# First expert layer of a two-layer adaLN kernel: indirect transfers without the waits on the shared expert

## The reference

```python
def _L0_ffn_ref(x, up, gate, down, router, w_up_s, w_gate_s, w_down_s):
    x_ = x.reshape(b * t, c)
    logits = x_ @ router.T
    idx = jnp.argmax(logits, axis=-1)            # one of 8 experts per token
    ...
    h = jax.nn.silu(g) * u                       # 256 hidden features per expert
    ye = jnp.einsum('ebh,ech->ebc', h, down)
    y = jnp.einsum('ebc,be->bc', ye, onehot)     # the token's own expert
    ys = jax.nn.silu(x_ @ w_gate_s.T) * (x_ @ w_up_s.T) @ w_down_s.T   # shared expert
    return (y + ys).reshape(b, t, c)
```

## Time and profile before

| | us |
|---|---|
| median of 3 runs | 1029.12 |
| the runs | 1025.5, 1029.12, 1032.63 |
| the profiled execution, its own time | 1024.61 |
| its span, first to last instruction | 1022.8 |
| mean granted TensorE clock | 0.978 of full speed |

### The profile page before, as it was taken

One profiled execution on the slowest core, in us unless ns is written; L12 is line 12 of the kernel. 1 busy time (PEld: TensorE's weight loads), 2 busy tenths in 40 slices (PEclk: granted clock), 3 DMA queues, 4 the chain that ended last, 5 costly groups with the idle time before them and its releaser, 6 DMA issues.

```text
span 1022.8 us, 21590 instructions
## 1 busy us (share of the span) xinstructions
PE 940.9 (92%) x7416; PEld 605.7 (59%) x7416; DVE 637.5 (62%) x2103; ACT 554.9 (54%) x1078; POOL 453.8 (44%) x682
## 2 busy tenths in 40 slices
PE   8999999999989989999994988889997999999996
PEld 3566777777654223334642886456664644499994
DVE  4789998999816967854642444768773643344444
ACT  6536667676657555565421554567775522255551
POOL 1146776777642946610064553045551044323331
PEclk9999999999999989999997999999999899999999
DMA  6600000000020000040012234000000010111115
GB/s 215 221 2 3 3 2 2 3 2 3 2 93 1 0 1 1 0 165 0 4 48 65 72 83 169 17 2 2 2 2 1 1 32 29 48 44 50 49 32 175
DMA packets 32602, 42.02 MB, mean 41 GB/s; under 512 B 6960, under 2 KB 26800, under 8 KB 31632
## 3 DMA queue, kind: packets, MB, share of 16 engines
q1 hardware_dynamic: 27952, 31.26, 9.8%
q0 software_dynamic: 4544, 9.38, 2.8%
HBM read 29.16 MB, written 16.66 MB: 45 GB/s over the span
## 4 chain that ended last, share of the span: by engine, by line
PE 72%; issue 14%; ACT 5%; DVE 5%; DMA 2%; POOL 1%; SPq 0%; DVEq 0%; POOLq 0%; ACTq 0%
PE PS L693 6%; PE PS L434 5%; PE PS L476 5%; PE PS L676 5%; PE PS L683 5%; PE PS L447 4%; PE PS L330 3%; PE PS L339 3%; PE PS L629 3%; PE PS L627 3%; PE PS L636 2%; PE PS L536 2%; PE PS L427 2%; PE PS L802 2%; PE PS L783 2%
## 5 line engine op out<-in xcount | busy, mean ns | idle before, releaser
L911 ACT ACTIVATE pw<-PS 128x384 f32<-128x384 f32 x256 | 111.5, 488 | 71.5 <-PE PS L456 68.9
L1587 POOL TENSOR_SCALAR_AFFINE_SELECT pw<-pw 128x256 f32<-128x256 f32 x256 | 105.1, 434 | 75.0 <-ACT pw L911 73.1
L1185 DVE CUSTOM_DVE_ANT_0 PS<-PS,above 128x256 f32<-128x256 f32 x256 | 115.8, 452 | 23.0 <-PE PS L427 22.8
L1653 POOL DMA_INDIRECT token_rows<-xnb,slot_in x78 | 75.0, 962 | 119.3 <-ACT xnb L1014 112.9
L1639 POOL TENSOR_TENSOR XS<-XS,N 128x512 f32<-128x512 f32 x64 | 81.2, 1288 | 55.4 <-DVE N L1263 34.7
L434 PE MATMUL PS<-kf,qm 32*128 32x256 f32 x512 | 103.6, 426 | 0.5 <-POOL qm L1596 0.5
L1439 DVE TENSOR_TENSOR rsb<-sqb,PS 128x256 f32<-128x256 f32 (+1 forms) x78 | 43.3, 555 | 96.7 <-PE PS L683 39.4
L1609 POOL TENSOR_SCALAR_AFFINE_SELECT pw<-pw 128x256 f32<-128x256 f32 x128 | 56.1, 472 | 68.6 <-ACT pw L1059 68.6
L1187 DVE CUSTOM_DVE_ANT_0 PS<-PS,above 128x128 f32<-128x128 f32 x256 | 84.6, 331 | 0.0
L1596 POOL TENSOR_SCALAR qm<-qs,qmask 128x256 f32<-128x256 f32 x64 | 59.7, 934 | 44.2 <-ACT kf L892 44.2
L997 ACT ACTIVATE sqb<-PS 128x512 f32<-128x512 f32 x48 | 28.7, 597 | 90.2 <-PE PS L627 80.3
(11 more groups left out here) (213 smaller groups left out, 2383.5 us busy)
## 6 DMA issues: line engine op xcount, KB each, us to landing
sorted_rows<-empty_rows_dram SPq DMA_DIRECT2D x2, 2535.0 KB, 14.4
slot_in<-sorted_rows SPq DMA_DIRECT2D x78, 65.0 KB
N<-token_rows SPq DMA_DIRECT2D x16, 256.0 KB, 4.6
X<-xT_dram SPq DMA_DIRECT2D x8, 256.0 KB, 5.7
ATT<-gate_dram SPq DMA_DIRECT2D x1, 2048.0 KB
XS<-down_dram SPq DMA_DIRECT2D x1, 2048.0 KB
H<-up_dram SPq DMA_DIRECT2D x1, 2048.0 KB
out_dram<-X SPq DMA_DIRECT2D x8, 256.0 KB, 3.6
```

The lines of the kernel that those rows point to most:

```text
L911: nc.scalar.activation(pw[:, w % 2, j + n, :], PS[:, A_PST + (2 * v + n) % 3, 0:3 * P], ACT.Exp).then_inc(a_p, 1)
L1185: nc.vector.tensor_tensor_reduce(x[:, 0:SEQ], x[:, 0:SEQ], above[:, :], 1.0, -3e38, ALU.add, ALU.max, mx[:, t // 8 % 2, 1, j, g:g + 1])
L1587: m = nc.gpsimd.affine_select(x[:, :, SEQ * k:SEQ * k + P], x[:, :, SEQ * k:SEQ * k + P], [[0, 2], [1, P]], ALU.is_ge, 0.0, base=0, channe ...
L1653: nc.gpsimd.indirect_dma_start(token_rows[l][:, :], bass.IndirectOffsetOnAxis(slot_in[:, r, D:D + 1].bitcast(mybir.dt.int32), 0), slot_out ...
```

## The change

In the first layer (l is 0) the 32 indirect transfers no longer wait for `s_hidden`. In the second (l is 1) the waits are as they were. The waits for `pos` and for the fill of `sorted_rows`, ahead of the loop, stay in both.

```diff
                 pool.wait_ge(q["pos"], 1)
                 pool.wait_ge(r_fill, 32)
                 for n in range(TILES):
-                    pool.wait_ge(q["s_hidden"], n * 7 // 8 + 3 if l else min(n * 2 // 3 + 1, NCH * c["NH"] + 2 - LATE))
+                    if l:
+                        pool.wait_ge(q["s_hidden"], n * 7 // 8 + 3)
                     nc.gpsimd.indirect_dma_start(sorted_rows[l][:, :], bass.IndirectOffsetOnAxis(pos[:, n:n + 1], 0),
                                                  rows[l][:, n, :], None).then_inc(q["dispatched"], 16)
```

## The result

| | before | changed |
|---|---|---|
| median, us | 1027.03 (6 runs) | 1038.58 (6 runs) |
| lowest to highest, us | 1024.24 to 1032.63 | 1034.91 to 1041.59 |
| profiled execution's span, us | 1022.8 | 1035.8 |
| ratio with its 95% interval | 1 | 1.0111 (1.0086 to 1.0137) |

The changed kernel is slower by 11.5 us where 4.4 us less was forecast. That is not the whole result. In one it takes 1023 to 1028 us and the sends of the first layer's routed part are about 1.75 us apart; in the other it takes 1014 to 1015 us and they are 1.44 us apart. I call them the **tight** and the **easy** condition. The traces of before and after above are of the tight one. In the easy condition the change makes the kernel faster, by 0.6% (0.9936, 0.9923 to 0.995), much as forecast.

What follows compares the result with a forecast made beforehand. The prediction took GpSimd's first-layer string of indirect transfers to set the time while TensorE idles 13.5 us; the median of 1029.12 us less 4.4 us, waits, side effects and clock at nothing, gave 1024.7 us, range 1018 to 1031.

Steps and rivals of the forecast that it cites:

- The string: GpSimd's 32 first-layer indirect transfers: without waits 1.265 us apart, last start at 548.26 instead of 552.69, gain 4.4 us.
- The third rival: First-layer waits cost more than thought, idle 0.30 us between transfers goes too: 13.7 us gain, 1015.4 us; chance 0.05.
- What is next: TensorE's transposition at line 667 starts at 552.5 instead of 556.95; its idle time falls from 13.5 to 9.1 us.
- Side effects of the earlier transfers: More transfers lie beside the first layer's shared expert, 27 instead of 24 before 543 us; cost nothing.
- The cover of 6.2 us: Before line 667's transposition: its other conditions are met by 546.3, it starts at 552.5; slipping shared steps have 6.2 us.
- The first rival: First layer's unpaced string slows, eighteen steps at 1.77 us: net 4.7 us slower, 1033.8 us; chance 0.06.
- The rule of the port pair: Skill's rule that VectorE holding the shared ports blocks GpSimd's descriptor writes, stretching the string; the sum took no stretch.
- The clock: TensorE's clock after its idle time before line 667: up to 1.6 us saved or lost, taken as nothing.

Runs made afterwards that it cites:

- x_plain: Changed kernel with the first layer's 32 transfers made plain ones in token order, sorting left out; 0.9926 of the kernel before, tight condition.
- z_spaced: Changed kernel with a GpSimd fill of 256 zeros per partition between the first layer's transfers; 1.0005 of the kernel before, tight condition.
- z_late: Changed kernel with the first layer's string started only when s_hidden is 8, then free; 1.0085 of the kernel before, tight condition.
- x_second: Kernel before with the second layer's transfers unpaced, the first layer's still paced; 1.0242 of the kernel before, tight condition.
- e8_half_pace: Kernel before with first-layer waits on s_hidden at n // 2 + 1 instead of min(2n/3 + 1, 16); 0.9998 of it, tight condition.

## Why the prediction was wrong

Point by point.

**The string.** Right. 39.4 us in both conditions, 2.3 us from the last start to the first slot's load. The third rival (the waits cost more) is out: spacing stayed at 1.265 us.

**What is next.** Right in the easy condition: 13.4 us of waiting became 9.0. There the kernel gains 0.6% (0.9936) and 0.55% (0.9945), 5.6 to 6.5 us against my 4.4. The traces show just the 4.4 us up to line 667 (48.0 to 43.6), so the last 1 to 2 us lie elsewhere; what they come from stays open. 4.4 us lies inside the interval of the second measurement and outside that of the first.

**Side effects of the earlier transfers: "Cost: nothing, by three rows."** This is the step that failed: a term that the sum put at 0 us came to 15 us. Up to line 667 the changed kernel was to gain 4.4 us, and it lost 10.9. I showed by the DMA share, by the bytes and by the distance of chosen multiplies that the unbroken string does not disturb the shared expert, and each of those rows is true. But I took the multiplies of 513 and 515 us, in the first 7 us of the string, and of 539 and 541, where it was paced, and left out the ones between. VectorE's multiply at 527.37 is 1.2 us late right behind the only 14 unbroken transfers that the trace has. In the tight condition ScalarE and VectorE start 1.4 to 13.4 us late from 16 to 19 us of unbroken string on, and the 14 steps end 22 us later, counted from the string's start (57.1 us behind it, where it was 34.6). The cover of 6.2 us that I named for such a slip was eaten several times over.

**The first rival** had the right place ("nothing measured beyond 14") and the wrong victim: I let the transfers slow each other down to 1.77 us. They never left 1.265. The price of 1033.8 us fell short of 1038.6. No rival let the string hold up the engines that compute. The row to follow was the late multiply at 527.37.

**The rule of the port pair.** The Trainium skill, page "SBUF — State Buffer", section "Who interferes with whom", says that where an instruction of VectorE contends with GpSimd, whoever issues first holds the shared port pair for the whole instruction and the other blocks, and that TensorE and ScalarE never wait on anyone. The trace after asks for something else. GpSimd keeps 1.265 us to the last transfer. ScalarE is idle for up to 13.40 us with its inputs ready. VectorE starts up to 4.1 us late, where GpSimd's instructions beside it take 0.96 us each. So the lock of that pair is not what these rows show.

**The clock.** The prediction took nothing for it; it took some 2 us here. The granted clock was 0.50 from 541 to 546 us and from 556 to 559 us. The first stretch is followed by TensorE's long wait and costs nothing. Behind the stop of 9.48 us, though, the three products from 555.93 to 560.47 took 4.54 us where 2.57 is usual. These 2 us follow from the stops and are part of the 10.9 us.

**What is shown and what is not.** Shown by single edits: the hold-up needs indirect transfers (x_plain), closer than 1.456 us at this length (z_spaced), for 16 to 19 us on end (z_late, x_second); it strikes in either layer, and pacing by the victims' own progress ends it (e8_half_pace). Shown by repeats: it comes with a condition of the machine that one chip had at one time and not at another, and that slows the first layer's sends as well. Not shown: what fills up in those 16 us, why ScalarE and VectorE are hit and TensorE is not, and what puts a machine in the tight condition. Above all one rival stands untested: all executions here were recorded by the profiler, and the strings that were held up are those whose signal records are largely missing. Either the signals themselves pile up, or their recording does and holds the engines; no kernel was timed without it. Until that is done, the loss in the tight condition is shown for the recorded kernel only.

**The better version.** The half pace (n // 2 + 1) takes 0.995 of before in the easy condition (the changed kernel 0.9945) and 0.9998 in the tight one (the changed kernel 1.0083). It beats the changed kernel where that loses, keeps its gain within the noise where that wins, and was in no measurement slower than before.

## What to carry to other kernels

A wait that paces a queue is flow control: before it is taken out, look for the first late instruction of any engine behind the longest unbroken stretch that the trace has, and read all instances of a repeated step there, not the tidy ones at both ends. If waiting is to be cut, set the waits so that they are met when all goes well and bite when the other engines fall behind. And measure a small change on more than one occasion: here its sign was that of the machine's condition. Where a trace lacks records that it should have, as the tight ones do, time the kernel without the recording before the loss is believed.

## What was not expected of the hardware

- The same program took 1014 or 1028 us by occasion; most of it (12 us) is the spacing of 39 indirect sends, 1.44 or 1.75 us. The second layer's sends were 2.76 us apart in both.
- GpSimd's plain transfers of 66 KB were issued every 0.54 us (17.23 us for 32), its indirect ones every 1.265 us.
- After the string, ScalarE and VectorE took 6 us more to recover (last issue at 550.11, on time again at 556.49).
- Completion signals of the whole kernel that the traces hold: 4910 to 4922 in the easy condition, 3442 to 3976 in the tight one, for the same transfers (5425 with the small loads added).
